# Planning and hops of a two-block graph kernel: descents summed first, table weights behind the plan, 14 key scatters behind the visit-row loads, extras' parts copied by ScalarE

## The reference

```python
def _rgcn_conv(x, src, dst, etype, bases_l, comp_l, root_l, bias_l):
    weight = jnp.einsum('rb,bio->rio', comp_l, bases_l)
    h = jnp.einsum('ni,rio->nro', x, weight)
    msg = h[src, etype]
    seg = dst * R + etype
    cnt = segment_sum(ones, seg, num_segments=N * R)
    norm = 1.0 / jnp.maximum(cnt[seg], 1.0)
    agg = segment_sum(msg * norm[:, None], dst, num_segments=N)
    return agg + x @ root_l + bias_l
# block 1: x = layernorm(x + three such layers, batch norm and relu between them)
# block 2: x = layernorm(x + (h + A h + A A h + A A A h) / 4 @ W_out + b_out)
#   h = x @ W_in + b_in
#   A h = segment_sum(h[dst] * (deg^-0.5[src] * deg^-0.5[dst]), src), deg counted over src
```

## Time and profile before

| | us |
|---|---|
| median of 3 runs (lowest, highest) | 5185.52 (5184.09, 5193.47) |
| profiled execution, its own time | 5210.32 |
| its span, first to last instruction | 5208.6 |
| mean granted TensorE clock | 0.811 of full |
| first key scatter / first gather of layer 0 | 160.02 / 378.03 |
| hops, from the first sums on | 4410.84 to about 5140 |

### The profile page before, as it was taken

How to read it: one execution, slowest core, us unless ns; L and a number is a source line. 1 busy time by engine, 2 the same in 40 slices (tenths; PEclk the granted TensorE clock), 3 DMA queues, 4 the chain that set the end, 5 groups by cost and what they waited for, 6 DMA issues and landing times.

```text
span 5208.6 us, 68902 instructions
## 1 busy us (share of the span) xinstructions
PE 3696.4 (71%) x16076; PEld 2010.5 (39%) x16077; DVE 3216.3 (62%) x8810; ACT 1086.7 (21%) x1906; POOL 2705.4 (52%) x2646
## 2 busy tenths in 40 slices
PE   7116766777678576777776687767767766999996
PEld 3003333333333344444444434444444443454443
DVE  6965455444434666666666646666666667747475
ACT  4000000000003233333333433333333334000000
POOL 0666677667661566666666426666666661000000
PEclk9556666566668788888888898888888888999998
DMA  6011111111115344444444354444444443999995
GB/s 230 14 32 46 45 46 46 46 46 47 45 46 211 93 124 123 123 123 124 124 123 125 116 219 122 122 123 124 121 123 123 124 123 113 368 347 364 338 360 195
DMA packets 416740, 717.16 MB, mean 138 GB/s; under 512 B 98579, under 2 KB 322632, under 8 KB 416111
## 3 DMA queue, kind: packets, MB, share of 16 engines
q1 hardware_dynamic: 332138, 545.45, 29.8%
q0 software_dynamic: 84096, 166.09, 12.5%
q10 hardware_dynamic: 130, 1.20, 0.1%
HBM read 432.25 MB, written 280.06 MB: 137 GB/s over the span
## 4 chain that ended last, share of the span: by engine, by line
PE 53%; issue 18%; POOL 9%; DVE 7%; another core or an unknown queue 7%; DMA 4%; ACT 1%; SPq 1%; DVEq 0%; ACTq 0%; POOLq 0%
PE psum L953 21%; PE psum L1003 11%; PE psum L940 9%; PE psum L929 6%; POOL area L622 6%; PE psum L901 3%; POOL key_list L592 3%; DMA area<-msg_table,visit_src 2%; DMA area<-counts 1%; PE psum L916 1%; PE psum L1016 1%; ACT bufE L672 1%; DVE edge_area L1181 1%; PE psum L1017 1%
## 5 line engine op out<-in xcount | busy, mean ns | idle before, releaser
L622 POOL DMA_INDIRECT area<-msg_table,visit_src x2490 | 2525.0, 1014 | 1427.7 <-issue 608.5
L953 PE MATMUL psum<-area 128*128 128x256 f32 x4980 | 1917.3, 487 | 374.8 <-DMA area<-msg_table,visit_src 143.7
L953 PEld LDWEIGHTS psum<-area 128*128 128x128 f32 x4980 | 1087.0, 238 | 972.2 <-issue 626.9
L1681 DVE TENSOR_TENSOR agg_and<-agg_and,psum 128x256 f32 x1245 | 520.8, 418 | 1160.5 <-PE psum L953 566.6
L672 ACT CAST bufE<-psum 128x512 f16<-128x512 f32 x1507 | 860.4, 587 | 1674.6 <-remote 713.1
L940 PE MATMUL psum<-bufE,carry 128*128 128x512 f16 x1505 | 647.1, 430 | 726.7 <-issue 612.5
L1650 DVE TENSOR_SCALAR area<-iota,agg_and 128x256 f32<-128x256 f32 x2490 | 886.4, 417 | 17.4 <-issue 15.8
L929 PE MATMUL psum<-bufE 128*128 128x512 f16 x1507 | 638.9, 424 | 0.9 <-issue 0.9
L1003 PE MATMUL psum<-area,edge_area 128*64 128x512 f16 (+1 forms) x5733 | 618.9, 371 | 27.0 <-DMA area<-counts 17.2
L940 PEld LDWEIGHTS psum<-bufE,carry 128*128 x1505 | 158.2, 105 | 1138.2 <-issue 1053.5
L1657 DVE TENSOR_SCALAR bufE<-iota,bufD 128x128 f16<-128x128 f16 x1507 | 432.7, 287 | 264.8 <-PE psum L929 147.4
(11 more groups left out here) (334 smaller groups left out, 1648.3 us busy)
## 6 DMA issues: line engine op xcount, KB each, us to landing
area<-counts SPq DMA_DIRECT2D x252, 896.0 KB, 6.8
counts<-bufE SPq DMA_DIRECT2D x1507, 128.0 KB
msg_table<-area SPq DMA_DIRECT2D x147, 512.0 KB, 2.6
area<-msg_table,visit_src POOLq DMA_INDIRECT x2490
agg_and<-counts SPq DMA_DIRECT2D x165, 128.0 KB, 6.7
area<-counts SPq DMA_DIRECT2D x21, 224.0 KB, 3.8
bufE<-inv_sqrt SPq DMA_DIRECT2D x2, 1568.0 KB, 12.5
out<-cur SPq DMA_DIRECT2D x12, 256.0 KB
```

The lines of the kernel that those rows point to most:

```text
L622: g.indirect_dma_start(out=msg[:, n % MV, :], out_offset=None, in_=msg_table, in_offset=bass.IndirectOffsetOnAxis(ap=visit_src[:, v:v + 1] ...
L953: t.matmul(psum[:, banks[c % len(banks)], at:at + W2], msg[:, n % MV, :], visit_sel[:, n % SV, :], start=v % 2 == 0, stop=v % 2 == 1).then ...
L1681: v.tensor_tensor(to, to, psum[:, banks[c % len(banks)], at:at + W2], ALU.add).then_inc(visit_added, 1)
```

## The change

What it does, engine by engine:

- SP issues the edge arrays first and the tiles' last `dst` (with a semaphore of their own, `lasts_in`) before bases and `comp`. The bases of layer 1 are loaded right behind the table writes of layer 0, ahead of `list_rows`.
- TensorE runs the sum of descents ahead of the transposes, then `sum_ranks`, `edges_before` and `spread_blocks`, and only then the 49 table blocks and the root product.
- The vector engine starts with the descents; `make_weights(0)` stands behind `plan_visits`. `find_lasts` stands inside `pad_windows`, behind the 13 counts, and reads the integers directly.
- GpSimd issues 98 scatters (`EARLY`), the seven visit-row loads, and then the last 14 scatters.
- For each extra ScalarE loads the column into a register and copies the 192 columns of parts to one of two slots (`extra_parts`). TensorE loads no register there; it runs three products of 64 columns for each extra, in the halves lower, upper, lower, into one of four banks. The vector engine adds two results for each extra in place of three.

```diff
+EARLY = CHUNKS - 2 * (PAD - 1)
...
         def _(sp):
-            sp.dma_start(bases_sb[:, :, :], bases[0].rearrange("b i o -> i b o")).then_inc(bases_in, 16)
-            sp.dma_start(comp_sb[:, :], comp.rearrange("(a l) r b -> a (l r b)", a=1).to_broadcast([128, LAYERS * R * BASES])).then_inc(bases_in, 16)
             sp.dma_start(dst_i, dst.rearrange("(p c) -> p c", p=EP)).then_inc(edges_in, 16)
...
             for to, of in last_of_tiles(tile_last_i, dst, 1):
-                sp.dma_start(to, of).then_inc(edges_in, 16)
+                sp.dma_start(to, of).then_inc(lasts_in, 16)
+            sp.dma_start(bases_sb[:, :, :], bases[0].rearrange("b i o -> i b o")).then_inc(bases_in, 16)
+            sp.dma_start(comp_sb[:, :], comp.rearrange("(a l) r b -> a (l r b)", a=1).to_broadcast([128, LAYERS * R * BASES])).then_inc(bases_in, 16)
...
             table(0)
 
+            sp.wait_ge(weights_ready, 1)
+            sp.dma_start(bases_sb[:, :, :], bases[1].rearrange("b i o -> i b o")).then_inc(bases_in, 16)
             sp.wait_ge(keys_written, 16 * CHUNKS)
...
-            place_keys()
+            place_keys(range(EARLY))
             pool.wait_ge(visits_planned, 1)
             pool.wait_ge(rows_out, 16)
             for j in range(VB):
                 g.indirect_dma_start(out=runs[:, j, :, :].rearrange("p e w -> p (e w)"), out_offset=None,
                                      in_=visit_rows.rearrange("(t e) w -> t (e w)", e=128),
                                      in_offset=bass.IndirectOffsetOnAxis(ap=visit_tile[:, j:j + 1], axis=0)).then_inc(tiles_in, 16)
+            place_keys(range(EARLY, CHUNKS))
...
+                act.wait_ge(parts_ready, HG * hop + HG)
+                for e in range(NX):
+                    x = NX * hop + e
+                    column = act.value_load(extra_at[0:1, 0, e:e + 1], min_val=0, max_val=(NBLK - 1) * PARTS)
+                    if x >= 2:
+                        act.wait_ge(extras_used, x - 1)
+                    a.copy(extra_parts[:, x % 2, :], parts.rearrange("p b n -> p (b n)")[:, bass.ds(column, PARTS)]).then_inc(extra_parts_ready, 1)
...
             pe.wait_ge(constants, CONSTANTS)
+            pe.wait_ge(hist_ready, 1)
+            t.matmul(psum[:, 7, 0:1], ones[0:EP, :], upto_block[:, NBLK:NBLK + 1], start=True, stop=True).then_inc(base_ready, 1)
             pe.wait_ge(rows_in, 32)
...
-                            if x >= 2:
-
-                                pe.wait_ge(extras_folded, x - 1)
-                            column = pe.value_load(extra_at[0:1, 0, e:e + 1], min_val=0, max_val=(NBLK - 1) * PARTS)
-                            bank = 4 + 2 * (x % 2)
-                            t.matmul(psum[:, bank, :], flat[:, bass.ds(column, 2 * H)], extra_in[:, x % XR, :], start=True, stop=True)
-                            t.matmul(psum[:, bank + 1, :], flat[:, bass.ds(column + H, 2 * H)], extra_in[:, x % XR, :],
-                                     start=True, stop=True).then_inc(extras_used, 1)
+                            if x >= 4:
+
+                                pe.wait_ge(extras_folded, x - 3)
+                            pe.wait_ge(extra_parts_ready, x + 1)
+                            for i in range(3):
+                                half = slice(i % 2 * H, i % 2 * H + H)
+                                last = t.matmul(psum[half, 4 + x % 4, :], extra_parts[:, x % 2, i * H:(i + 1) * H], extra_in[:, x % XR, :],
+                                                start=i < 2, stop=i > 0)
+                            last.then_inc(extras_used, 1)
...
+            sum_ranks()
+            edges_before()
+            spread_blocks()
             pe.wait_ge(x_kept, NXT)
             pe.wait_ge(weights_ready, 1)
-            sum_descents()
-            table_blocks(0, xT, 0, NBLK // 3)
-            sum_ranks()
-            edges_before()
-            table_blocks(0, xT, NBLK // 3, NBLK)
+            table_blocks(0, xT, 0, NBLK)
             root_product(0, xT)
-
-            spread_blocks()
             spread_ends()
...
-            make_weights(0)
-            dve.wait_ge(edges_in, 96)
+            dve.wait_ge(edges_in, 64)
...
+                find_lasts()
                 whole = left[0:EP, w13].bitcast(I32)
...
             plan_visits()
+            make_weights(0)
...
-                    bank = 4 + 2 * (x % 2)
-                    fold(to[:, bass.ds(column, BW)], (psum[H:2 * H, bank + 1, :], psum[H:2 * H, bank, :], psum[0:H, bank, :]), extras_folded)
+                    fold(to[:, bass.ds(column, BW)], (psum[H:2 * H, 4 + x % 4, :], psum[0:H, 4 + x % 4, :]), extras_folded)
```

More of the change, by code:

```diff
@@ L290, in build @@
         rest = agg_and[:, NP + XR * 256:NP + XR * 256 + HB * H]
-        assert XR * 256 + HB * H <= COLS + 128 - NP
+        AT = NP + XR * 256 + HB * H
+        extra_parts = agg_and[:, AT:AT + PARTS].bitcast(BF16).rearrange("p (s n) -> p s n", n=PARTS)
+        assert AT + PARTS <= COLS + 128
         agg = agg_and[:, 0:NP]
@@ L304, in build @@
         psum = ctx.enter_context(nc.psum_tensor("psum", [128, 8, 512], F32))
[L307 removed]
+        edges_in, lasts_in, params_in, rows_in, bases_in = sem("edges_in"), sem("lasts_in"), sem("params_in"), sem("rows_in"), sem("bases_in")
         constants = sem("constants")
@@ L508, in _ @@
             for layer in range(1, LAYERS):
-                if layer == 1:
-                    sp.wait_ge(weights_ready, layer)
-                    sp.dma_start(bases_sb[:, :, :], bases[layer].rearrange("b i o -> i b o")).then_inc(bases_in, 16)
                 table(layer)
@@ L587, in _, with place_keys @@
             g.memset(norm[:, :], 0.0).then_inc(constants, 1)
-            def place_keys():
-                for k in range(CHUNKS):
+            def place_keys(chunks):
+                for k in chunks:
                     g.indirect_dma_start(out=key_list, out_offset=bass.IndirectOffsetOnAxis(ap=key_address[:, k:k + 1], axis=0),
@@ L766, in _ @@
                 last.then_inc(x_turned, 1)
-            def sum_descents():
-                pe.wait_ge(hist_ready, 1)
-                t.matmul(psum[:, 7, 0:1], ones[0:EP, :], upto_block[:, NBLK:NBLK + 1], start=True, stop=True).then_inc(base_ready, 1)
             def edges_before():
@@ L1216, in find_lasts @@
                 upto = in_bucket[:, 0:NBLK * PER].rearrange("p (n j) -> p n j", j=PER)
-                link(v.tensor_copy(block, tile_last[:, :, 1]))
-                link(v.tensor_scalar(block, block, 7, None, ALU.logical_shift_right))
+                dve.wait_ge(lasts_in, 32)
+                link(v.tensor_scalar(block, tile_last_i[:, :, 1], 7, None, ALU.logical_shift_right))
                 link(v.tensor_copy(tile_block[:, :], block))
@@ L1290, in rank_link @@
                     dve.wait_ge(rank_step, ranked[0])
+                dve.wait_ge(lasts_in, 32)
+                rank_link(v.tensor_copy(tile_last[:, :, :], tile_last_i[:, :, :]))
                 rank_link(v.tensor_copy(payload[:, :, 1], dst_i))
@@ L1308, in _ @@
                 dve.wait_ge(lasts_reloaded, 32)
-            find_lasts()
+                rank_link(v.tensor_copy(tile_last_i[:, :, 1], tile_last[:, :, 1]))
             link(v.tensor_scalar(bucket_i, src_i, LOW_BITS, None, ALU.logical_shift_right))
```

5 lines of the change are left out of this document (1 added, 4 removed).

## The result

Four runs of the changed kernel took 5115.69 us in the median (5099.84 to 5120.01), beside four of the kernel before with 5187.19 us: 71.5 us less by the medians. The ratio, taken over all of these runs and so not quite that of the medians, is 0.9855, or 75 us (95% interval 0.9832 to 0.9878, that is 63 to 87 us). The forecast said 46.5 us less, and its own range of 5128 to 5146 us lies above the result. The profiled execution took 5116.7 us with a span of 5115.0.

A forecast was written before the change was run, and what follows sets the result against it. It read matmuls and gathers of the three visit layers, untouched, as 42% of the chain, with GpSimd's scatters ahead and the DMA bounding the hops. From 5185.5 us, 41.6 (setup) and 5 (extras) off gave 5139, range 5128 to 5146.

The forecast's parts named there:

- The extras: Hops: pairs of extras 5.79 us apart lose wide products and register loads on TensorE; 5 us gained.
- I take the DMA's end, since the share is of this very mix: Hops: DMA at share 1.00 and 366 GB/s holds a pair to 5.73 us, so 5 us gained, not 38.
- The sign that the forecast named: Hops: if right, pairs 5.7 us apart with waits on the loads of counts.
- Rival (a): Hops: the DMA has room and TensorE sets the pace; gain 20 to 38, likeliest 30 us, 5114 in all; chance 0.20.
- TensorE's own floor: Hops: six half-width products stream two at a time, 48 x 0.111 = 5.3 us a pair, 38 us gained over 82 pairs.
- Early start: Setup: first step behind the branch at 20.7 us in place of 50.53, first scatter at 130.0, 30.0 us earlier.
- Weights behind the plan: Setup: make_weights(0) takes 9.9 us before the grouping of edges, which starts at 145.4 us, 20.1 us earlier, not 30.
- Table and its cover: Setup: layer 0's table and root product end at 246.5 us, spread_ends needed at 267.7; 21 us of cover, costing nothing.
- Rival (c): Setup: clock stays at half, the table comes late, first gather at 408 us, kernel slower at 5210; chance 0.04.
- Scatters: Setup on GpSimd: 98 scatters take 170.7 us plus 2.3, then a wait for visit rows until 306.7; first gather at 336.4.
- rival (b): Setup: scatters slow down beside the table's writes, 0.43 us more each for some 55, 24 us, 5163 in all; chance 0.12.
- The layers: Visit layers: untouched by the change; the forecast is wrong if they change length by more than 10 us.

The follow-up runs named there:

- E1: The kernel before with only the extras' part of the change (copies, 64-column products, two-step fold); 5145.97 against 5176.79 us, ratio 0.9944.
- E5: The kernel before with extras' loads, behind the first of each slot, bringing only the left half of their columns; ratio 0.9993.
- E8: The changed kernel with the extras' six half-width products a pair cut to 64 of 512 columns each; ratio 0.9829.
- E6: The changed kernel with ScalarE's copies kept, but the extras' products wide (128 columns of parts) and the third addition as before; ratio 0.9912.
- E4: The changed kernel with the 3.2 MB node feature load held back on SP until the vector engine has counted the windows; 5099.48 us, ratio 0.9848.
- E9: The changed kernel with TensorE's sum of the descents behind the transposes again; ratio 0.9902.
- E10: The changed kernel with make_weights(0) and the loads of its bases in front of the edges again; ratio 0.9865.
- E3: The changed kernel with all 112 key scatters ahead of the visit-row loads; ratio 0.9888.
- E12: The changed kernel with E4's held-back feature load and E10's order of the weights; 4703.42 us, ratio 0.9843.
- E2: The changed kernel with the extras' part undone, leaving the setup's part alone; 5137.22 us, ratio 0.9928.
- E7: The changed kernel with a register load that nothing uses in front of each extra's products on TensorE; ratio 0.9866.

## Why the prediction was right or wrong

**The extras: wrong, and this is most of the miss.** The step that failed is "I take the DMA's end, since the share is of this very mix". It took the share of 1.00 at 366 GB/s as a ceiling, 5.73 us a pair, and let 5 us remain of a TensorE gain of 38. The pairs came 5.43 us apart and the hops gave 30.4 us; E1 and E5 settle that the DMA was no bound. The sign that the forecast named, waits on the loads of counts, is missing: in the window of the earlier trace rows no engine waits for such a load, which could have been read before, and none does in the changed kernel. With a ring of loads always in flight the share reads 0.98 to 1.03 at 348, 366, 390 and 408 GB/s alike. The loads became the bound at 408 (E8).

Rival (a) was right in its reason (a load lands 6.9 us after its issue and is needed 8.6 us later, so TensorE sets the pace). That its likeliest 30 us met the 30.4 is luck: they came from the DMA too, 363 GB/s at a share of 0.94 made 386 at a full one, 5.43 us a pair. The loads can do 5.14 (E8); the 5.43 that was measured is TensorE's.

The forecast set the Trainium skill's page SBUF — State Buffer, with about 358 GB/s from HBM to a core, beside the row. The Trainium skill's page HBM Reference, section "Specifications (TRN2)", says that this is the share of a core when both of a pair stream, and that one alone measures well above it, near 425 GB/s. The 390 and 408 GB/s of these traces agree with that second sentence; whether the other core of the pair was idle no run shows.

TensorE's own floor was sized 0.1 us too low: 5.3 us a pair forecast, 5.43 measured, which makes 30 us of the 38. Of the gain per pair, 0.36 us, E6 puts 0.13 on the register addresses and 0.23 on the halves. The forecast's rule of thumb that six halves stream two at a time fits that: four wide products took 4 x 0.215, three pairs of halves 3 x 0.215, a difference of 0.215. That nothing else lies behind the 0.23 is not shown: in E6's trace a wide product starts 0.31 us behind the half product before it, and a half product 0.31 behind the wide one, where two wide ones stand 0.216 apart, so each change of width takes some 0.09 us, twice a pair. The changed kernel has no such changes; what it loses in their place no run separates.

**Early start: mechanism right, size 4 us too large.** Edges at 12.9 us (forecast 13.0) and the sign test at 16.6 (near 17) came out. Failed: "L1209 to the first step behind the branch 4.06 us". That was measured at 46 us, when the DMA moved almost nothing. At 16.6 us the load of the node features was under way, and it took 8.07 us. I counted each queue that the edges were moved past, but not the instruction packets, which stand in no line of the program. With the load held back (E4) the step starts at 20.75 us and the first scatter at 129.96, the forecast's 20.7 and 130.0. E9 confirms the rest: with the sum late again 23.0 of the 26.1 us by which the first scatter had come earlier went.

**Weights behind the plan: right in length, idle in worth.** They took 9.7 us (139.4 to 149.1; forecast 9.9), and the grouping started at 149.12, near the forecast 145.4 and the 4 us of the branch. E10 shows that the forecast should have asked for the alternative: it would have had 340.0 instead of 341.6 us.

**Table and its cover: right.** The root product ended at 248.6 us (forecast 246.5) and L1380 ran at 270.17 (forecast 267.7), so 21 us of cover came out as 21.5. Rival (c) did not happen: the granted clock was 0.97 from 149.3 to 237 us, though TensorE had all but rested from 60 to 148 us at a clock of 0.50.

**Scatters: right.** 98 scatters in 173.2 us (170.7 and 2.3 forecast) at 159 GB/s of traffic in place of 10: rival (b) is out. GpSimd waited 3.50 us for the visit rows, forecast some 4. The rows landed 11.5 us behind the last step, not 10.9, and the last 14 scatters took 22.2 us to the first gather, not 20.9; with the 4 us of the branch these are the 5.2 us between 336.4 and 341.6. E3 shows that the split is worth 10.6 us.

**The layers.** "I am wrong if the layers themselves change length by more than 10 us": they did, by 11 and 16 us in the two profiled executions, and it meant nothing. Over the profiles of before, the changed kernel and E1 to E4 layer 1 took 1261.5 to 1283.5 us and layer 2 1300.1 to 1320.8, and E1, with the setup of before, has the shortest layer 2. In the group of E5 to E8 the time from the first gather to the first hop sum was 4037.1 us with the setup of before (E5) and 4038.4, 4043.1 and 4038.1 with the changed one (E6 to E8).

**The sum.** 36.4 where 41.6 stood, 30.4 where 5 stood: 66.8 us by the traces instead of 46.6, and 71.5 by the medians. The two errors have opposite signs: the setup gave 5 us less than forecast, the hops 25 more.

## What to carry to other kernels

A DMA share of 1.00 is no bound while the loads are issued ahead: ask first whether the consumer ever waits for a load, and halve the bytes to be sure. What stands in the way of a skipped branch can be the fetch of the code behind it; keep large loads out of that moment. When work is moved off one path, look at which path it lands on: here GpSimd waited for exactly what had been put ahead of the visit rows.

## What the runs showed of the hardware

- A skipped branch on the vector engine cost 3.9 to 4.3 us, from the sign test to the next step, with the DMA almost idle (kernel before 4.06, E4 4.14, E12 3.93, E5 4.31), and 8.0 to 8.1 us with the 3.2 MB load under way (changed kernel, E2, E10). In the gap there are one or two instruction packets of 0.01 MB; the difference lies ahead of them (E4).
- The same 16 DMA engines at a share near 1.00 moved 348 (E5, with smaller loads), 366 (before), 376 (E6) and 390 GB/s (changed), as fast as TensorE took the loads, and 408 GB/s (E8) where the loads were the bound.
- Products whose weights' address comes from a register left gaps of 0.18 to 0.39 us on TensorE at 7 of 26 pairs, 0.13 us a pair in the mean (before); a register load without such a use left none (E7).
- Setup and hops took the same time to a few us in all groups of runs (hops of the changed kind 704.5 to 709.8 us), but the visit layers did not: 1220.7, 1272.5 and 1304.5 us in the changed kernel, 1097.4, 1129.7 and 1170.0 in E9. The record names one chip for the group of E1 (kernel before 5176.79 us) and for that of E12 (4778.89), so that the chip makes the difference is not shown. In layers 1 and 2 the granted clock tells the two apart, in layer 0 hardly:

```profile
375.00:1440.00 1065.00, 853.65 (x1991) 403.71 (x1992) 569.56 (x1425) 0.00 (x0) 816.48 (x816) 0.64 0.19 51
1700.00:2700.00 1000.00, 781.54 (x3056) 384.00 (x3054) 746.38 (x2472) 400.04 (x683) 754.45 (x730) 0.97 0.46 136
```

(E9) against the changed kernel's

```profile
1700.00:2903.00 1203.00, 862.03 (x3334) 509.14 (x3332) 826.76 (x2752) 415.21 (x727) 829.97 (x805) 0.85 0.42 124
```

Why layer 0, at a clock of 0.64 against 0.62, took 123 us less in E9's group, no run settles.
